# Decoder layer on one core: the calls of all engines in another order, at the head, in the slots and at the tail

## What is computed

```python
Q, K, V = x @ Wq.T + bq, x @ Wk.T + bk, x @ Wv.T + bv
scores_cross = einsum(einsum(Q, W_cross), K)       # 16 heads
scores_conv  = einsum(Q, einsum(M, K))             # M: banded shift weights
scores = (gt * scores_cross + (1.0 - gt) * scores_conv) * scale   # gt = sigmoid(gate)
out = softmax(where(causal, scores, -inf)) @ V
x = layernorm(x + out @ Wo.T + bo)
...
scores = (x @ w_q.T) @ (ctx @ w_k.T).T / sqrt(16)  # ctx: 375 rows for each batch
attn = softmax(where(mask == 0, -1e9, scores))
x = layernorm(x + (attn @ (ctx @ w_v.T)) @ w_o.T)
...
def fp4_linear(x, w):                              # blocks of 16, scale = max|.| / 6
    return fp4_quant_dequant(x) @ fp4_quant_dequant(w).T
h = silu(fp4_linear(x, w_gate)) * fp4_linear(x, w_up)   # 704 wide
x = layernorm(x + fp4_linear(h, w_down))
```

## Time and profile before

| | us |
|---|---|
| median of 3 runs | 631.72 |
| lowest, highest | 630.38, 638.22 |
| the profiled execution | 637.13 |
| its span, first to last instruction | 635.1 |
| PE busy | 548.7 (86%) |
| DVE busy | 511.7 (81%) |
| ACT busy | 286.0 (45%) |
| POOL busy | 177.0 (28%) |

### The profile page before, as it was taken

One profiled execution on the slowest core, in us unless ns is written; L12 is line 12 of the kernel. 1 busy time (PEld: TensorE's weight loads), 2 busy tenths in 40 slices (PEclk: granted clock), 3 DMA queues, 4 the chain that ended last, 5 costly groups with the idle time before them and its releaser, 6 DMA issues.

```text
span 635.1 us, 16505 instructions
## 1 busy us (share of the span) xinstructions
PE 548.7 (86%) x5698; PEld 354.0 (56%) x5698; DVE 511.7 (81%) x1444; ACT 286.0 (45%) x671; POOL 177.0 (28%) x251
## 2 busy tenths in 40 slices
PE   3777677769989999999999998898999998888875
PEld 2544344546566666657566656564665664544543
DVE  3388767867898989899999997576989896786994
ACT  1242235446445455555554555454455554443421
POOL 7013141325122333324241413141232324211201
PEclk9998689899999999999999998897999999997998
DMA  8266552544363362627263536354352625320000
GB/s 246 56 194 180 156 157 82 148 115 134 96 180 106 110 172 79 193 78 201 83 174 85 177 95 177 102 141 135 106 164 80 189 72 149 88 83 17 32 1 25
DMA packets 75934, 77.14 MB, mean 121 GB/s; under 512 B 13069, under 2 KB 67405, under 8 KB 75853
## 3 DMA queue, kind: packets, MB, share of 16 engines
q1 hardware_dynamic: 73612, 73.75, 40.7%
q10 hardware_dynamic: 2240, 2.35, 1.3%
HBM read 39.89 MB, written 27.00 MB: 105 GB/s over the span
## 4 chain that ended last, share of the span: by engine, by line
PE 47%; DVE 27%; issue 9%; DMA 7%; ACT 4%; SPq 3%; POOL 2%; DVEq 0%; POOLq 0%; ACTq 0%
PE misc L2243 15%; PE misc L2229 7%; DVE junk L1430 5%; PE score L2159 4%; PE prob L2168 3%; PE misc L2284 2%; PE prob L2174 2%; PE xpv L2218 2%; DVE xden L1469 2%; PE apv L2206 2%; DVE amax L1422 2%; DVE qt L1347 2%; PE misc L2329 2%; DMA xden<-xoT 2%; PE score L2135 2%
## 5 line engine op out<-in xcount | busy, mean ns | idle before, releaser
L1430 DVE CUSTOM_DVE_ANT_0 junk<-score,maskbias 112x375 bf16<-112x375 f32 x256 | 129.0, 542 | 36.5 <-PE score L2159 35.2
L931 ACT ACTIVATE xP<-prob 128x448 f32<-128x448 f32 (+1 forms) x192 | 94.0, 541 | 57.9 <-PE prob L2174 57.6
L2243 PE MATMUL misc<-wguT,xqT 128*128 128x352 f32 x224 | 82.6, 498 | 1.9 <-ACT xqT L891 1.1
L2159 PE MATMUL score<-xK,xQ 64*128 64x375 f16 x256 | 44.7, 335 | 20.9 <-DVE xmax L1430 18.5
L740 POOL TENSOR_TENSOR move_a<-mT,eye 128x448 bf16<-128x448 bf16 x32 | 36.1, 1147 | 77.9 <-ACT mT L891 77.9
L764 POOL TENSOR_TENSOR rstd<-veps,half 128x1 f32<-128x1 f32 (+1 forms) x44 | 28.2, 640 | 98.8 <-DVE veps L1505 98.8
L740 POOL TENSOR_TENSOR move_x<-mT,eye 128x448 bf16<-128x448 bf16 x32 | 33.1, 1040 | 78.1 <-ACT mT L891 78.1
L2243 PEld LDWEIGHTS misc<-wguT,xqT 128*128 128x128 f32 x224 | 40.1, 197 | 26.4 <-issue 9.7
L760 POOL TENSOR_TENSOR aattT<-anum,aden 128x224 f32<-128x224 f32 x16 | 10.7, 670 | 157.7 <-DVE aden L1469 122.3
L2243 PE MATMUL misc<-xwvT_s,ctxT_s 128*128 128x256 f32 (+1 forms) x192 | 51.4, 401 | 3.1 <-DVE ak_parts L1449 2.1
L2271 PE MATMUL misc<-ctxT_s,xwkT_s 128*128 128x375 f32 x128 | 50.2, 516 | 2.9 <-DVE bq_s L1389 2.9
(11 more groups left out here) (156 smaller groups left out, 1089.6 us busy)
## 6 DMA issues: line engine op xcount, KB each, us to landing
xk_dram<-xk_parts SPq DMA_DIRECT2D x64, 192.0 KB, 3.2
xK<-xk_dram SPq DMA_DIRECT2D x16, 768.0 KB, 4.5
ctxT_s<-in_ctxT SPq DMA_DIRECT2D x15, 375.0 KB, 3.7
aq_dram<-aq_parts SPq DMA_DIRECT2D x64, 64.0 KB, 2.2
ak_dram<-ak_parts SPq DMA_DIRECT2D x64, 64.0 KB, 2.2
aQ<-aq_dram SPq DMA_DIRECT2D x16, 256.0 KB, 2.9
aK<-ak_dram SPq DMA_DIRECT2D x16, 256.0 KB, 2.9
xq_dram<-xq_parts SPq DMA_DIRECT2D x64, 64.0 KB, 2.1
```

The lines of the kernel that those rows point to most:

```text
L931: act.activation(xP[0:KEYS[c], g % 2, c], prob[m][0:KEYS[c], 0:GH * S].rearrange("p (h q) -> p h q", h=GH), ACT.Exp).then_inc(probs.taken[ ...
L1430: dve.tensor_tensor_reduce(junk[:, m], score[m][0:S, 0:SC], maskbias[:], 1.0, -3.0e38, ALU.add, ALU.max, xmax[:, b.par, h // (2 * GH), h / ...
L2159: pe.matmul(score[m[a]][:, 0:SC], xQ[rows_, b.par, at, :], xK[rows_, b.par, at, 0:SC], start=True, stop=True).then_inc(scores.full[m[a]], 1)
L2243: mm = pe.matmul(misc[m][0:rows_, 0:cols], actT(c), weightT(c), start=(c == 0), stop=(c == DT - 1))
```

## The change

The same calls are made with the same arguments, in another order, on all five engines. No call is added or taken away. In the slots these move:

- SP: `put_q` goes to the front, `put_k` behind both `spread`, the read of aQ between them, `store` ahead of `put_x1`, and `next_x` to the end of the slot.
- POOL: `residual(a)` goes from behind `attend(a, 0)` to between the two `diagonal(i, a, ...)`.
- ACT: `ctxk_hi(0)` comes ahead of `ctxv(0)`, and `layernorm(ft, 2)` goes behind the maxima of X.mT.
- DVE: `quant_h(i, f, 0, 6)` goes behind `max_cross(i, c, 7)`; `max_cross` 2 and 3 come one small piece earlier; `quant_h(i, f, 0, 4)` and the second `gate_` come ahead of `max_cross` 4.
- PE: `scores_cross(i, c, 5)` comes behind the three `pv_cross(i, p, 1, ...)`.

In the head and the tail many calls of each engine change places, mostly by one to four positions. In the lists of the PSUM rings, `1:q` and `1:k` change places in `MISC_IN`, and `14:V2` and `14:A.q` in `MISC_OUT`; the rest of the lists is only wrapped differently.

```diff
@@ -631,31 +632,31 @@
                 kv = i + 1
                 p = i - 1
                 ft = tile(i - 1)
-                put_k(i, fr)
-                next_x(i)
+                put_q(i, fr)
                 next_ctx(i)
-                put_q(i, fr)
                 next_xT(i)
                 spread(a, 0)
+                get(fr, aq_dram, aQ, aq_out, aq_in, apv_done)
                 spread(p, 1)
-                get(fr, aq_dram, aQ, aq_out, aq_in, apv_done)
+                put_k(i, fr)
                 get(fr, ak_dram, aK, ak_out, ak_in, apv_done)
                 put_xk(kv)
                 put_xq(i, a)
                 get(kv, xk_dram, xK, xk_out, xk_in, xpv_done)
                 get(a, xq_dram, xQ, xq_out, xq_in, xpv_done)
-                put_x1(a)
                 if ft:
                     store(ft)
+                put_x1(a)
+                next_x(i)
...
@@ -838,9 +839,9 @@
                 xo = tile(i + 1)
                 ft = tile(i - 1)
                 diagonal(i, a, 0, False)
+                residual(a)
                 diagonal(i, a, 1, False)
                 attend(a, 0)
-                residual(a)
                 if ft:
                     power(2, ft)
...
@@ -1808,35 +1809,34 @@
                 max_cross(i, c, 0)
                 if ft:
                     residual_ffn(i, ft)
+                    moments(i, ft, 2, "down", 0)
                 max_cross(i, c, 1)
-                if ft:
-                    moments(i, ft, 2, "down", 0)
                 if f:
                     gate_(i, f, 0)
+                max_cross(i, c, 2)
                 if ft:
                     moments(i, ft, 2, "down", 1)
-                max_cross(i, c, 2)
                 if f:
                     up(i, f, 0)
                 if ft:
                     moments(i, ft, 2, "down", 2)
                 if f:
                     quant_h(i, f, 0, 0)
-                    quant_h(i, f, 0, 1)
                 max_cross(i, c, 3)
                 if f:
+                    quant_h(i, f, 0, 1)
                     quant_h(i, f, 0, 2)
                     quant_h(i, f, 0, 3)
+                    quant_h(i, f, 0, 4)
+                    gate_(i, f, 1)
                 max_cross(i, c, 4)
-                if f:
-                    gate_(i, f, 1)
                 invert(a, 0)
                 if f:
                     up(i, f, 1)
                 max_cross(i, c, 5)
                 if f:
+                    quant_h(i, f, 0, 5)
                     quant_h(i, f, 1, 0)
-                    quant_h(i, f, 0, 4)
                 max_cross(i, c, 6)
                 if f:
                     quant_h(i, f, 1, 1)
...
@@ -1854,24 +1852,23 @@
                 ctxk_lo(i, kv, 0)
                 ctxk_lo(i, kv, 1)
                 if f:
-                    quant_h(i, f, 0, 6)
                     quant_h(i, f, 1, 4)
                 max_cross(i, c, 7)
                 if xo:
                     residual_cross(i, xo)
                 if f:
+                    quant_h(i, f, 0, 6)
                     quant_h(i, f, 1, 5)
                     quant_h(i, f, 0, 7)
                 if xo:
                     moments(i, xo, 1, "X.o", 0)
                 if f:
                     quant_h(i, f, 1, 6)
+                if xo:
+                    moments(i, xo, 1, "X.o", 1)
                 xq_lo_(i, a)
                 if f:
                     quant_h(i, f, 0, 8)
-                if xo:
-                    moments(i, xo, 1, "X.o", 1)
-                if f:
                     quant_h(i, f, 1, 7)
                 if xo:
                     moments(i, xo, 1, "X.o", 2)
...
@@ -2574,10 +2571,10 @@
                 turned_cross(i, p, 1, 2)
                 if f:
                     gate_up(i, f, "up", 1)
-                scores_cross(i, c, 5)
                 pv_cross(i, p, 1, 0)
                 pv_cross(i, p, 1, 1)
                 pv_cross(i, p, 1, 2)
+                scores_cross(i, c, 5)
                 ctx_k(i, kv, 0)
                 scores_cross(i, c, 6)
                 project_self(i, a)
...
-                quant_weight(6, 2)
-                quant_weight(6, 3)
-                ctxk_lo(at[2], at[3], 0)
-                max_self(at[2], at[3], 1)
                 max_self(at[2], at[3], 2)
                 max_self(at[2], at[3], 3)
-                quant_weight(6, 4)
-                q_lo(at[2], at[4])
-                quant_weight(6, 5)
+                max_cross(at[2], at[2], 0)
                 quant_weight(6, 6)
-                quant_weight(6, 7)
-                max_cross(at[2], at[2], 0)
                 max_cross(at[2], at[2], 1)
                 max_cross(at[2], at[2], 2)
                 max_cross(at[2], at[2], 3)
                 max_cross(at[2], at[2], 4)
+                ctxk_lo(at[2], at[3], 0)
                 max_cross(at[2], at[2], 5)
                 max_cross(at[2], at[2], 6)
                 max_cross(at[2], at[2], 7)
-                quant_weight(6, 8)
+                invert(at[3], 0)
                 max_self(at[3], at[4], 0)
...
                 front(at[2], at[4], "k")
+                scores_cross(at[1], at[1], 0)
                 pv_cross(at[1], at[0], 0, 2)
                 turned_self(at[1], at[2], 0)
-                scores_cross(at[1], at[1], 0)
-                front(at[2], at[4], "v")
                 scores_cross(at[1], at[1], 1)
                 turned_cross(at[1], at[0], 1, 0)
                 pv_self(at[1], at[2], 0)
                 scores_cross(at[1], at[1], 2)
                 turned_self(at[1], at[2], 1)
-                scores_cross(at[1], at[1], 3)
+                front(at[2], at[4], "v")
                 pv_self(at[1], at[2], 1)
                 turned_cross(at[1], at[0], 1, 1)
+                scores_cross(at[1], at[1], 3)
+                turned_cross(at[1], at[0], 1, 2)
                 pv_cross(at[1], at[0], 1, 0)
...
@@ -1298,10 +1299,10 @@
                 tanh(at[16], at[12], 1)
                 take(at[17], "X.xT", xqT[:], DT, P)
                 tanh(at[17], at[13], 0)
+                layernorm(at[11], 2, y[:, at[11].par])
                 tanh(at[17], at[13], 1)
+                take(at[17], "hT0", hqT[:, 0:4], 4, P)
                 hT1(at[17], at[12])
-                layernorm(at[11], 2, y[:, at[11].par])
-                take(at[17], "hT0", hqT[:, 0:4], 4, P)
                 hT1(at[18], at[13])
                 take(at[18], "hT0", hqT[:, 0:4], 4, P)
                 layernorm(at[12], 2, y[:, at[12].par])
```

445 lines of the change are left out of this document (223 added, 222 removed), and 12 rows, old and new, of tables (MISC_IN, MISC_OUT).

## The result

The changed kernel takes 641.15 us (median of four runs, 640.2 to 643.15), the kernel before 634.87 over the four runs taken by then: ratio 1.0107, 95% interval 1.0062 to 1.0152. It is about 1% slower, where 624.8 us was forecast, in a range of 614 to 632.5. The kernel before varies more from one execution to the next than I had allowed for: 629.3 to 640.2 us in 25 runs, with mean granted clocks between 0.945 and 0.975.

The account below looks back on a forecast made before the run. It took PE and DVE, handing work to each other, as the bound. From 637.13 us, −3.5 (slots), −1.8 (head) and −1.7 (tail) gave 630.1; times 0.9915, 624.8 us, range 614 to 632.5.

Parts of the forecast that it names:

- A slot in all ... I take 0.35 us.: Steady slots: 0.43 + 0.25 us of PE waits could go, about 0.35 returns; net gain 0.35 us a slot.
- The wait that I let come back at hT1: Steady slots, PE's turn of hq: about 0.35 of the 0.43 us gained at X.mT could return as a wait.
- The term for ten slots: Slots 4 to 13: ten slots at 0.35 us each, −3.5 us (0 to −10).
- An op that has to wait it out is some 0.3 to 0.4 us shorter.: Slots, DVE's xq op: waiting out xres (0.73 us) instead of one move_a (1.13) shortens it by 0.3 to 0.4 us.
- I cost it at nothing: Slots, x_s asked for at the slot's end: POOL waits up to 1.5 us, with no cost on PE.
- SP in the slots.: Slots, SP's put_k behind spread(p, 1): aK lands at 321.7, PE reads it at 323.83; cover 2.1 us, cost nothing.
- The rival on the slower side: aK late at PE's first scores_self of a slot: 1 us excess costs 10 us, 635; chance 0.10, including similar resources.
- Other moves (front v, put_x1, the first quant_weight rows) I take as +0.3.: Head: the remaining moves cost 0.3 us, for a v on PE that now comes ahead of pv_self.
- Head: −1.8 us (−3.7 to +0.9).: Head: −0.9 for aattT in slot 1, −1.2 for slot 2's first cross maxima, +0.3 for other moves.
- Both moves that I had picked: Head: pv_self(1,2,1) ahead of slot 1's fourth cross-score pair, −0.9; slot 2's first cross maxima ahead of two wd ops, −1.2.
- Tail: −1.7 us (0 to −3.4).: Tail: three PE waits, 1.05, 1.15 and 1.15 us, about halved by earlier h quantization on DVE and ACT's new order.
- The clock gives more back.: Rival, whole kernel: more evenly fed PE regains a third of 22.9 us of missing full clock, 7.6 us, giving 617.2; chance 0.26.

Follow-up runs that it names:

- slots_only: The kernel before with only the ten steady slots in the new order, on all five engines; ratio 0.9996 (0.9965 to 1.0027).
- head_only: The kernel before with only the head (ramp) in the new order, on all five engines; 645.6 us, ratio 1.0190 (1.0148 to 1.0232).
- tail_only: The kernel before with only the tail (drain) in the new order, on all five engines; ratio 1.0022 (0.9989 to 1.0054).

## Why the prediction was wrong, step by step

- **"A slot in all ... I take 0.35 us."** The size was right (33.60 to 33.25), and so was the fall at X.mT, 0.75 to 0.31. The reasons were only half right. The wait that I let come back at hT1 did not come; the moves that I "costed at nothing" (gate_ ahead of max_cross 4, scores_cross 5) cost 0.1 us in one company, and in another DVE's, PE's and ACT's lists gave 0.16 together. The rest, 0.20 us, is the late x_s, which I had costed at nothing; that the sum of the two came out at the 0.35 that I took is luck. The term for ten slots was right where the time at 1.2 GHz didn't move (3.8 us in slots_only against 3.5); the changed kernel gave 6.1 us in slots 5 to 13, up to 3.4 of it by the clock.
- **"An op that has to wait it out is some 0.3 to 0.4 us shorter."** This is a price that was wrong by its sign. Behind xres stands the second move_a, and xq waits out both: 1.82 us, not 0.8. In the changed kernel this never shows, only because of the next step.
- **"I cost it at nothing" (x_s at the end of the slot).** I worked out a wait of POOL of up to 1.5 us and wrote that DVE's xq "would even run clear of POOL". It does (0.84 us of wait, 0.43 us for xq), and the slot's gain hangs on it. What I didn't ask is what the same move does behind the last slot: 3.8 us of wait on POOL, 0.94 of it on PE. It isn't shown to have made the tail longer.
- **"SP in the slots."** Right: the read of aK is issued at 324.68, lands 2.6 us later, and PE reads it at 330.31. The rival on the slower side was put there, on the one queue position whose margin I had worked out, and had 0.10.
- **"Other moves (front v, put_x1, the first quant_weight rows) I take as +0.3."** This is the step that cost the forecast. SP's head was laid out anew in some forty lines, and I priced none of them. The late read of xK of batch 4 alone cost 5.2 us in slot 4, and the new head alone, in head_only, makes the kernel 1.9% slower.
- **"Head: −1.8 us (−3.7 to +0.9)."** Apart from xK, measured +1.5 in the changed kernel's own profile and +4.7 to +6.2 in the four other traces with the new head. This is the term of the sum that failed, with xK as its largest single part. Both moves that I had picked do in their place what I said. The wait for aattT in slot 1 is gone (1.79 to under 0.2 us), and in slot 2 the maxima start 1.9 us sooner behind the turn of the self maxima (127.38 behind 124.96, against 128.21 behind 123.89). The L1346 step on 704 elements behind the first pair took 1.36 us, not 0.9. The pairs then run no faster, and from the X.mT of slot 2 to the next turn it takes 6.2 us in place of 5.2. Single waits taken away in a chain that waits at over twenty places bought nothing, and why the head got longer over all stays open.
- **"Tail: −1.7 us (0 to −3.4)."** Measured +2.0 in the profile, outside; +2.9 in the first part and −0.9 in the rest, where the three waits are. I had taken three waits of the last 40 us and not looked at the 32 us at the tail's start, where PE waits for ACT's exponentials once pv_cross no longer stands ahead. By its time the new tail alone is undecided (1.0022, 0.9989 to 1.0054).
- **"The clock gives more back."** The mean went from 0.964 to 0.957. The kernel before runs at 0.945 to 0.975 by itself, so this rival could not have been decided by one profile. I also wrote that the slow stretches lie at the ends, from two rows; 13.7 us at 1.2 GHz lie between 387 and 439 us of the same trace, in slots 10 and 11 with 0.4 us ahead of them.

The common fault: I priced the moves that I could see a reason for, as gains, and took the rest as nothing. The diff puts in some 250 lines and takes out as many, and the rest was the larger part of them.

## What to carry to other kernels

When a list written out by hand is laid out anew, compare each queue's position of the loads whose margin is small, in the head too, where every batch is a special case: one read that was issued 13 us later cost 5.2 us here, more than the 3.8 us that the ten slots of slots_only gave. A steady loop's gain can be read from one period; a head's can't, and its range has to reach further to the slower side than one from picked moves does. Where two engines share a port, look at what stands directly behind the op that holds it, since a waiting op may have to sit out both.

## What the runs showed of the hardware

A two-input DVE op on SBUF that takes 0.43 us alone took 1.14 us beside one POOL tensor op and 1.82 us beside two that followed each other without a gap. A gap of 0.84 us on POOL was enough for it to get through. The Trainium skill ("SBUF — State Buffer", "Who interferes with whom") calls the pair of ports that VectorE and GpSimd share an exclusive lock, and says that a VectorE instruction with two SBUF inputs contends with a GpSimd instruction that reads SBUF. These rows agree, and add that the waiting DVE op did not come next when POOL's op ended.

PE's clock fell to 1.2 GHz during pauses of PE (at 201.4 us in the changed kernel, in its 3.26 us of waiting; at 543.9 us in tail_only, in its 1.97 us), but it fell at other times in executions of the same kernel, and the time moved with it: slots_only ran from 629.1 to 638.1 us in ten runs.
